# Attention of a vision tower moved by sixteen slots of the pipeline, and the experts' weighing moved to VectorE

## The reference, cut to what matters

```
h = attention(x)                                # per window of 64 tokens: softmax(q k^T) v, then @ proj_w.T + proj_b
h = layernorm(h)                                # n
h = h_att + n + mamba(n)                        # h_t = exp(delta_t A) h_{t-1} + (x_t delta_t) B_t ; y_t = C_t . h_t
f = layernorm(h)
logits = softmax(relu(f @ rw1 + rb1) @ rw2 + rb2); top_w, top_i = top_k(logits, 2); w = softmax(top_w)
e_out = relu(relu(f @ w1[e] + b1[e]) @ w2[e] + b2[e]) @ w3[e] + b3[e]      # each of 6 experts
out = h + sum over the two chosen e of w_e * e_out
```

## Time and profile before

| what | value |
|---|---|
| median of three runs | 1782.14 us |
| profiled execution, its span | 1766.49 us, 1764.7 us |
| busy share PE, DVE, ACT, POOL | 74%, 70%, 61%, 69% |
| first scan begins | 203.6 us |
| iterations 4 to 12 | 95.6 us each |
| last scan begins | 1686.2 us |
| granted TensorE clock, mean | 0.852 |

### The profile page before, as it was taken

How to read it: one execution, slowest core, us unless ns; L and a number is a source line. 1 busy time by engine, 2 the same in 40 slices (tenths; PEclk the granted TensorE clock), 3 DMA queues, 4 the chain that set the end, 5 groups by cost and what they waited for, 6 DMA issues and landing times. The chain is left out here.

```text
span 1764.7 us, 25944 instructions
## 1 busy us (share of the span) xinstructions
PE 1304.8 (74%) x7988; PEld 605.8 (34%) x7988; DVE 1243.5 (70%) x1611; ACT 1084.0 (61%) x2036; POOL 1219.9 (69%) x1619
## 2 busy tenths in 40 slices
PE   3665768687877878696868777787869686667565
PEld 1442525243343424252434333342425242122121
DVE  1211478878787888878787888888887878778830
ACT  1235466757667676767576767767676757565522
POOL 2013276877868788878778787878887877878642
PEclk9887879898888989898989989898989898677755
DMA  2000578765867776767767677767676777779810
GB/s 69 1 16 30 133 177 250 188 201 154 223 175 203 194 201 187 217 176 191 213 173 221 180 219 188 206 188 206 189 203 188 195 208 197 211 209 242 223 36 6
DMA packets 214689, 303.75 MB, mean 172 GB/s; under 512 B 78924, under 2 KB 79128, under 8 KB 214424
## 3 DMA queue, kind: packets, MB, share of 16 engines
q1 hardware_dynamic: 214552, 302.09, 62.1%
HBM read 274.75 MB, written 20.97 MB: 168 GB/s over the span
## 5 line engine op out<-in xcount | busy, mean ns | idle before, releaser
L1215 POOL TENSOR_TENSOR hc<-hs,c_rep 128x512 f32<-128x512 f32 x512 | 654.6, 1280 | 228.1 <-DVE hs L1011 226.3
L1011 DVE TENSOR_TENSOR_SCAN hs<-bank,state,xd 128x512 f32<-128x512 f32 x512 | 651.4, 1275 | 50.8 <-issue 35.9
L758 ACT ACTIVATE bank<-dl,a_neg 128x512 f32<-128x512 f32 x512 | 351.2, 687 | 71.3 <-DMA dl<-delta_rows 35.2
L1002 DVE TENSOR_TENSOR xd<-xd,bank 128x512 f32<-128x512 f32 x512 | 336.1, 661 | 30.3 <-DMA xd<-xdel_rows 19.3
L1029 DVE TENSOR_REDUCE neg_max<-bank 128x8 f32<-128x512 f32 x128 | 88.1, 688 | 194.6 <-PE bank L521 194.5
L766 ACT ACTIVATE probsT<-bank 128x512 f32<-128x512 f32 x128 | 76.4, 597 | 228.1 <-PE bank L532 228.1
L521 PE MATMUL bank<-k_heads,q_diag 128*128 128x512 f32 x256 | 163.2, 723 | 50.9 <-DMA q_diag<-rot 25.7
L531 PE MATMUL bank<-q_diag,k_heads 128*128 128x128 f32 x1024 | 190.7, 309 | 11.1 <-ACT shift L751 11.1
L531 PEld LDWEIGHTS bank<-q_diag,k_heads 128*128 128x128 f32 x1024 | 168.9, 200 | 87.0 <-issue 81.3
L444 PE MATMUL bank<-hc,wts 128*32 128x512 f32 x1024 | 190.6, 800 | 4.4 <-POOL hc L1215 3.0
L689 PE MATMUL bank<-e,wts 64*64 64x512 f32 x384 | 80.7, 920 | 109.9 <-ACT e L936 109.9
(11 more groups left out here) (159 smaller groups left out, 2249.7 us busy)
## 6 DMA issues: line engine op xcount, KB each, us to landing
xd<-xdel_rows SPq DMA_DIRECT2D x512, 256.0 KB, 4.4
dl<-delta_rows SPq DMA_DIRECT2D x512, 256.0 KB, 4.0
delta_rows<-delta SPq DMA_DIRECT2D x16, 512.0 KB, 7.2
xdel_rows<-xdel SPq DMA_DIRECT2D x16, 512.0 KB, 5.2
xin<-in_x_dram SPq DMA_DIRECT2D x32, 128.0 KB, 2.6
q_diag<-rot SPq DMA_DIRECT2D x32, 128.0 KB
out_dram<-res SPq DMA_DIRECT2D x256, 16.0 KB
k_heads<-rot SPq DMA_DIRECT2D x128, 16.0 KB
```

The lines of the kernel that those rows point to most:

```text
L758: act.activation(decay_ps[n % 2][:, :], dl[:, n % 4, :], ACT.Exp, scale=a_neg[:, g:g + 1])\
L1002: dve.tensor_tensor(xd[:, n % 8, :], xd[:, n % 8, :], b_ps[:, :], ALU.mult).then_inc(injected.sem, 1)
L1011: dve.tensor_tensor_scan(hs[:, n % 4, :], decay_ps[n % 2][:, :], xd[:, n % 8, :], state[:, u:u + 1], ALU.mult, ALU.add).then_inc(scanned.s ...
L1215: pool.tensor_tensor(hc[:, n % 8, :], hs[:, n % 4, :], c_rep[:, BAND * h:BAND * h + BAND], ALU.mult)\
```

## The change

Attention of chunk c+3 now begins in slot 24 of iteration c and ends in slot 23 of iteration c+1: windows' steps 9 to 27 fall on slots 1 to 19. Normalization of a chunk takes slots 24 to 31 of iteration c and slot 0 of the next, numbered r = 0 to 8, beside the next chunk's attention steps. Slots of the scan, of `prepare`, of `route` and of the expert layers stay. The DMAs for keys and queries move from slots 12 and 13 to 28 and 29, the load of x from slot 4 to slot 20; x of chunk 0 is loaded third in the setup. VectorE multiplies the hidden layer by the weight straight from PSUM in slots 25 to 30; ScalarE's copy and GpSimd's multiplication are gone; the third layer comes one slot earlier (27, 29, 31).

```diff
@@ -205,7 +205,6 @@
         e1 = sb("e1", [128, 2, 512])
-        wb = e1
         ew = sb("ew", [128, 2 * EP, 512])
@@ -261,7 +260,6 @@
         route_act = sig("route_act", 2)
-        weighed = sig("weighed", 2 * EP)
         stored = sig("stored", 16 * 16)
@@ -284,7 +282,12 @@
-            return (c + 3, n - 8) if n >= 8 else (c + 2, n + 24)
+            return (c + 3, n - 24) if n >= 24 else (c + 2, n + 8)
+
+        def normalized_at(c, n):
+
+
+            return (c + 2, n - 24) if n >= 24 else (c + 1, n + 8)
@@ -369,11 +372,11 @@
                     if has(c + 3):
-                        if n == 4:
+                        if n == 20 and past(c + 2):
                             load(c + 3)
-                        if 12 <= n < 14:
-                            heads(c + 3, 4 * (n - 12), 4 * (n - 11))
-                        if n == 13:
+                        if 28 <= n < 30:
+                            heads(c + 3, 4 * (n - 28), 4 * (n - 27))
+                        if n == 29:
                             queries(c + 3)
@@ -386,6 +389,7 @@
             sp.dma_start(once[:, 0:N_ONCE], packed[:, N_KEPT:N_KEPT + N_ONCE]).then_inc(loaded, 16)
+            load(0)
             at = SEL["w_sel"][0]
@@ -636,7 +640,7 @@
                                   start=True, stop=True)
-                for e, slot in enumerate((28, 30, 32)):
+                for e, slot in enumerate((27, 29, 31)):
                     if n == slot:
@@ -692,7 +696,7 @@
                 use = F["outT"]
-                pe.wait_ge(weighed.sem, weighed.at(k, 2 * e + 2))
+                pe.wait_ge(W[f"wb_{e + EP}"].drained, W[f"wb_{e + EP}"].empty(k))
                 for s in range(2):
@@ -800,14 +804,14 @@
-            def normalize(k, n):
-                if n == 11:
+            def normalize(k, r):
+                if r == 3:
                     act.wait_ge(ln1_pool.sem, ln1_pool.at(k, 2))
                     act.activation(sq[:, :, :], cen[:, :, :], ACT.Square, scale=ROOT).then_inc(ln1_act.sem, 1)
-                if n == 15:
+                if r == 5:
                     act.wait_ge(ln1_dve.sem, ln1_dve.at(k, 2))
                     inv_root(k, st_a, 2, 0, 3, 4, ln1_act, 2)
-                if n == 24:
+                if r == 7:
                     act.wait_ge(ln1_pool.sem, ln1_pool.at(k, 8))
@@ -909,13 +913,6 @@
                     act.activation(st_f[:, 14, :], st_f[:, 13, :], ACT.Exp).then_inc(route_act.sem, 1)
-                if 25 <= n < 25 + 2 * EP:
-                    i = n - 25
-                    use = W[f"wb_{PAIRED[i]}"]
-                    act.wait_ge(use.filled, use.full(k))
-                    if i > 1 or past(k - 1):
-                        act.wait_ge(weighed.sem, weighed.at(k, i - 1))
-                    copy(wb[:, i % 2, :], use.bank[:, :]).then_inc(use.drained, 1)
                 if n == 23:
@@ -978,8 +975,9 @@
                         prepare(c + 1, 1 - odd, n)
-                    if has(c + 2):
-                        normalize(c + 2, n)
+                    k, r = normalized_at(c, n)
+                    if has(k):
+                        normalize(k, r)
@@ -1048,9 +1046,9 @@
-            def normalize(k, n):
+            def normalize(k, r):
                 st, done = st_a, ln1_dve
-                if n == 8:
+                if r == 0:
                     use = A["proj"]
@@ -1058,10 +1056,10 @@
                        .then_inc(use.drained, 1)
-                if n == 9:
+                if r == 1:
                     dve.wait_ge(A["proj"].drained, A["proj"].empty(k))
                     dve.tensor_reduce(st[:, 0, :], hid[:, :, :], X_AXIS, ALU.add).then_inc(done.sem, 1)
-                if n == 13:
+                if r == 4:
                     dve.wait_ge(ln1_act.sem, ln1_act.at(k, 1))
@@ -1088,6 +1086,11 @@
                     route(k, n)
+                if 25 <= n < 25 + 2 * EP:
+                    j = PAIRED[n - 25]
+                    use = W[f"wb_{j}"]
+                    dve.wait_ge(use.filled, use.full(k))
+                    dve.tensor_tensor(ew[:, j, :], ew[:, j, :], use.bank[:, :], ALU.mult).then_inc(use.drained, 1)
                 if n == SLOTS + 3:
@@ -1236,18 +1240,18 @@
-            def normalize(k, n):
-                if n == 10:
+            def normalize(k, r):
+                if r == 2:
                     pool.wait_ge(ln1_dve.sem, ln1_dve.at(k, 1))
                     center(k, hid, st_a, cen, ln1_pool)
-                if n == 23:
+                if r == 6:
                     pool.wait_ge(ln1_act.sem, ln1_act.at(k, 4))
                     scale(k, cen, st_a[:, 6, :], lnx, ln1_pool)
-                if n == 25:
+                if r == 8:
                     pool.wait_ge(ln1_act.sem, ln1_act.at(k, 7))
@@ -1285,11 +1289,6 @@
                 route(k, n)
-                if 26 <= n < 26 + 2 * EP:
-                    i = n - 26
-                    j = PAIRED[i]
-                    pool.wait_ge(W[f"wb_{j}"].drained, W[f"wb_{j}"].empty(k))
-                    pool.tensor_tensor(ew[:, j, :], ew[:, j, :], wb[:, i % 2, :], ALU.mult).then_inc(weighed.sem, 1)
```

## The result

The changed kernel takes 1919.35 us (median of 4 runs, 1916.69 to 1942.85), the kernel before in the same session 1779.34. The ratio is 1.082, 95% interval 1.072 to 1.091: clearly slower, where 1755 us was forecast. Ratios leave out runs over 1.5% above the fastest of their kernel, and so can differ from the quotient of two medians, by 0.9 points at most here (e1). The profiled execution has a span of 1915.0 us against 1764.7, 150.3 us more.

A forecast was written before the change was run, and what follows sets the result against it. No engine was full over the whole run; the bound changed by slot range (GpSimd, TensorE, ScalarE, or none). Terms -38.5 + 12 + 3.8 + 0.4 - 5 = -27.3 on 1766.5 gave 1739, scaled 1755 us; range 1705 to 1805.

The forecast's parts named there:

- Filling: Before the first scan and in iteration 0: fewer attention pairs come first, so iteration 1 begins earlier, -38.5 us.
- The weighing's price: VectorE's multiplications in slots 25 to 30: 0.66 us each, with ends of 0.6 and 1.9.
- the new loop through one bank: Slots 24 to 29: TensorE's weights' matmuls wait for VectorE's multiplication; VectorE's scan and feed (1.9 us) were to cover it.
- the far end of my bounds: VectorE's weighing slowed by GpSimd, up to 1.9 us a pass; the bounds were 0 to 7.5 us an iteration.
- The end: After the last scan: the third layer's 3.95 us wait for GpSimd and about 1 us of weighings go, -5.
- The steady iteration: Iterations 1 to 12, summed by slot range from the fullest engine's busy time: +1.0 us each, +12 in all.
- the 3.50 us wait: Slots 20 to 23: VectorE's wait before a small routing step, forecast to shrink to 2 us without the windows.
- iteration 13: Keeps its windows to slot 19, lacks four rotations: 94 us where it took 90.20, +3.8.
- Rival 4: Coupling waits in dense slots 1 to 13 and the new loop cost 3 us an iteration: 1779 us, chance 0.08.
- Rival 3: Filling gives back half, as silu, softplus and tables hold ScalarE ahead of shift and exp: +18, 1773 us, chance 0.12.
- Rival 2: TensorE goes cold in slots 20 to 31, enters dense ones slow: +7 us an iteration, 1827 us, chance 0.18.
- Rival 1: The steady iteration gets shorter too, by 2.5 us: 1712 us, chance 0.2.

The follow-up runs named there:

- e1: The kernel before with VectorE's weighing of the experts alone, attention still at slot 8: ratio 0.983, 1767.4 us.
- e16: The changed kernel with SiLU and its two table loads left out, a copy of eight columns in their place: ratio 1.018, 1817.89 us.
- e6: The changed kernel with the maxima put behind scan and feed on VectorE: ratio 1.077.
- e15: e1 with SiLU and its two table loads left out, a copy of eight columns in their place: ratio 0.989.
- e4: The changed kernel with the router's exp put ahead of the last hidden layer's output in slot 21 on ScalarE: ratio 1.058.
- e2: The changed kernel with the weighing put back on ScalarE and GpSimd, the third layer's slots with it: ratio 1.080.
- e12: e1 with x of the first chunk loaded first and the router's exp ahead of the last expert layer's output: ratio 0.985, 1751.6 us.
- e8: The changed kernel with three useless matmuls added on TensorE, one in slot 20 and two in slot 21: ratio 1.098.

## Why the prediction was wrong, point by point

**Filling, right.** The first scan came at 163.69 (165 forecast) and iteration 1 began at 255.91 (254.7). The first maximum of chunk 2 came at 174.20, where I had taken 173.51 over from rows 6 (how far such times vary stands in the last section):

```profile
163.69 1.28 DVE L1009 TENSOR_TENSOR_SCAN hs<-bank,state,xd 128x512 f32<-128x512 f32 x1 [0.93 <-ACT bank L762]
...
174.20 0.68 DVE L1027 TENSOR_REDUCE neg_max<-bank 128x8 f32<-128x512 f32 x1
```

That the first scan was met to 1.3 us is partly luck: in the runs with attention at slot 24 it comes anywhere from 163.3 (e16) to 179.2 us (e6), and with attention at slot 8 from 203.6 to 222.9. x first brought 1.5 us and not 1.1: TensorE began at 16.27 instead of 17.81.

**The weighing's price, right.** 0.681 us mean (L1093 above) for 0.66. GpSimd is no longer full in slots 24 to 31, 16.40 us of 26.26 (16.3 forecast). The 39.1 us that L1093 stands for L661 are about 0.4 us a pass; that is the new loop through one bank, 1.49 us of it in one place above, and it was not covered as I had said. A slowdown by GpSimd, the far end of my bounds, did not come.

**The end, right in kind.** -8.6 us for -5. Iteration 15, for which I had no term, gave 3.7 of it back; e1 has the same length there and behind its last scan, so both belong to the weighing. The third layer behind the last scan stands 0.78 us where it stood 3.95:

```profile
1845.27 0.64 PE L702 MATMUL bank<-ew,wts 128*64 128x512 f32 x1 [0.78 <-DVE ew L1093]
```

**The steady iteration, wrong: this is the step that failed.** I moved each step's busy time and then took the fullest engine as the length of a slot range. The sum gave +1.0 us an iteration; measured were +14.3. Most busy sums were close: in slots 8 to 13 I had ScalarE 18.0 (measured 18.47), VectorE 14.6 (13.99), TensorE 18.7 (17.05); in 24 to 31 VectorE 22.9 (22.47), GpSimd 16.3 (16.40); in 20 to 23 VectorE 10.1 (9.78). TensorE's were not where its clock was low: 12.18 for 8.1 in slots 20 to 23 (clock 0.66), 18.66 for about 14 in 24 to 31 (0.87). It was the fullest engine of neither forecast range. The lengths of the ranges came out so:
- slots 0 to 3 and 14 to 19: 9.95 and 18.12 us for 9.8 and 17.7. Here the forecast held, though in the second no engine is full (GpSimd, the fullest, 15.92).
- slots 8 to 13: 23.42 for 20.3. Fullest was ScalarE with 18.47, and in e16, relieved of 4.5, the range takes 16.69. The sum treats ScalarE's 4.5 us in one piece as if they could lie anywhere in the range. They stand between a `pv` copy and its PSUM bank, and scores, maximum and scan are chained behind it. Shown by e16 against e15.
- slots 20 to 23: 17.29 for 12.0. I let the 3.50 us wait shrink to 2, as no windows are left in front. It grew to 4.79; the last hidden layer runs at half clock as before, and two scans wait for ScalarE's decay besides, 1.49 us (in the rows above) and 0.94. e4 shows the exp's place in it: 2.6 us an iteration, (1326.0 - 1295.1) / 12.
- slots 4 to 7: 14.80 for 13.0, TensorE full as forecast, the size a little low: 14.80 busy for 13.1, with a clock of 0.89 that I had put at 1.00.
- slots 24 to 31: 26.26 for 23.7. VectorE is at 22.47 as forecast, plus 1.73 us for the projection, 0.57 for the second keys and 1.49 for the weights' matmul.
- iteration 13, which I made from the same sums: 106.0 us for 94, and iteration 14 83.9 for 79.6.

SiLU's hold is thus worth 6.7 of the 14.3 us an iteration, in the sense that leaving it out gives these back, and at slot 8 nothing. It is not the excess of one slot range: without it slots 8 to 13 are shorter than the 19.95 us of the kernel before, and against that kernel the changed one is longest in slots 24 to 31 (27.1 for 21.9, means of iterations 1 to 12) and 4 to 7 (15.2 for 11.2). The early exp is worth another 1.7 once SiLU is out (1245.7 against 1224.8 over 12 iterations), and about 6 are left in the dense slots 4 to 7 and in the waits of 24 to 31. Those I have read from rows; no run takes them away one by one, and their cause stays open. In e2, where GpSimd weighs, slots 24 to 31 take 22.9 us on average but slots 0 to 3 take 16.0 (10.7 in the changed kernel), so that loss only changes its place with the weighing.

**The rivals.** Rival 4, coupling waits in dense slots, had the right mechanism, a chance of 0.08 and a price of 3 us an iteration; the steady part lost more than four times that, some of it in slots 4 to 7 with TensorE full. Rival 3 had seen that SiLU and its tables hold ScalarE ahead of attention's steps, but I looked for it only while the pipeline fills, where it did no harm, and not in the 12 iterations where attention now stood in the same slots. Rival 2 gave the right sign and part of the reading: clock 0.66 in slots 20 to 23, 0.87 in 24 to 31, 0.84 in the whole iteration, and slots 20 to 31 took 43.55 us, where it gave about 41.7 (35.7 and 6). Its cause is neither shown nor ruled out there, since no run raised that clock. In slots 8 to 13, e16 brings the clock back to 1.00 by taking a wait away, so there the low clock followed from the wait. The Trainium skill, "TensorE: Matmul & The Clock Gate", on oscillation, describes bursts that wait for others and start at half clock; the two score rows, 1.13 and 2.07 us, agree. Rival 1 fell.

**Range and chances.** The range ended at 1805 because the edges of the steady part were made from the same sums of busy time, and no wait of several microseconds in every iteration stood among them.

## What to carry to other kernels

When a stage is moved along a hand-ordered pipeline, list for each of its steps what now stands directly ahead of it in each engine's queue, and above all the longest unbroken pieces (here 4.5 us of table load, SiLU, table load); a slot range's length is the longest chain through such places, and the fullest engine is only its lower bound. A piece that costs nothing at one place may cost more than its own length at another; here TensorE's clock was lower behind the wait (0.85 in slots 8 to 13, 1.00 without it), which is the likely reason, though no run separates it. The part of the change that does no harm is VectorE's weighing without the shift: 1767.4 us (0.983, 0.967 to 1.000), or with x first and the early exp 1751.6 (0.985, 0.975 to 0.995). Both are clearly faster than the changed kernel. Against the kernel before, the interval of the first reaches 1.000, so no gain is shown; that of the second does not, but its steady iterations are as long (1155.4 us for twelve, 1154.0 before).

## What the runs showed that I had not expected

Leaving out 4.5 us of one engine's work took 6.7 us out of an iteration at slot 24 and none at slot 8. And the filling varies between profiled executions with the same work in it (of different kernels, each profiled once). Up to the first scan the kernel before took 203.6 us, e1 222.9 and e12 221.9; the changed kernel took 163.7, e8 165.3 and e4 176.2. Much of the difference lies in attention running alone. In e1 a pair of windows takes 67.38 - 60.79 = 6.59 us, where the kernel before took 4.06, and its score matmuls take 2.07 us instead of 1.12:

```profile
60.79 2.07 PE L519 MATMUL bank<-k_heads,q_diag 128*128 128x512 f32 x2 [0.33 <-ACT pv L749]
...
67.38 2.07 PE L519 MATMUL bank<-k_heads,q_diag 128*128 128x512 f32 x2 [0.33 <-ACT pv L749]
```

These are the durations that scores have at the lower level of the clock (0.50 over the pair at 954.24 above), yet the windows view gives 1.00 over 62.90 to 69.49. That 1.00 is a blank: the clock records of e1's trace begin at 124.4 us, and the view shows 1.00 where there is none. In the traces the first record, of full clock, stands just ahead of the first pair that takes 1.12 us: 124.4 and 126.6 us in e1, 68.5 and 71.0 in e12, 43.5 and 46.2 in the kernel before, 42.1 and 44.7 in the changed one. So the score matmuls ran at half speed from the first pair (36 to 38 us) up to a moment that differs by 82 us between these executions. The level also falls again later: in e12 the second chunk's pairs take 2.07 us with a recorded clock of 0.50. Ahead of the first record the matmuls' durations tell the level, and one profile prices this filling no better than to some 20 us.
